# A two-layer sequence model: SiLU of B and C on ScalarE, store waits moved into the mixer's queue, row buffers set up earlier by GpSimd

## The reference

```
x = x + _L0_attn_ref(_layernorm(x), ...)      # decayed linear attention, gate, output product
x = x + _L0_ffn_ref(_layernorm(x), ...)       # router with top 8 of 64
x = x + _L1_attn_ref(_layernorm(x), ...)      # the mixer:
    proj = x @ in_proj_w.T                    # gate (8192), x (8192), B (1024), C (1024), dt (128)
    x, B, C = silu(causal depthwise conv of 4 taps + bias)
    L = exp(segsum(dt * A));  Y = (C B^T * L) @ (x * dt) + part of the earlier chunk + x * D
    out = (groupwise rms norm of Y * silu(gate)) @ out_proj_w.T
x = x + _L1_ffn_ref(_layernorm(x), ...)       # low-rank experts, top 16 of 64
```

## Time and profile before

| what | value |
|---|---|
| median of 3 runs | 2722.26 us (2721.75 to 2727.92) |
| the profiled execution, its time | 2725.14 us |
| the profiled execution, its span in the trace | 2723.4 us |
| TensorE matmul busy | 2566.6 us, 94% |
| VectorE, GpSimd, ScalarE busy | 69%, 54%, 50% |
| chain that ended last | TensorE 47%, VectorE 4%, "issue" 4%, GpSimd 2%, ScalarE 2% |

### The profile page before, as it was taken

How to read it: one execution, slowest core, us unless ns; L and a number is a source line. 1 busy time by engine, 2 the same in 40 slices (tenths; PEclk the granted TensorE clock), 3 DMA queues, 4 the chain that set the end, 5 groups by cost and what they waited for, 6 DMA issues and landing times.

```text
span 2723.4 us, 59094 instructions
## 1 busy us (share of the span) xinstructions
PE 2566.6 (94%) x19678; PEld 2041.8 (75%) x19678; DVE 1877.7 (69%) x2744; ACT 1349.5 (50%) x2481; POOL 1460.6 (54%) x1428
## 2 busy tenths in 40 slices
PE   4999999999999679799999999999999999999989
PEld 3778787787787456677777777777777777777777
DVE  5675666766757679757667777587576677775874
ACT  3434434434334255456564664665565646656621
POOL 1654655556546113457556656576575566575720
PEclk8999999999999879899999999999999999999999
DMA  2010010110110023211111111101111111111011
GB/s 89 24 50 29 32 46 24 40 40 23 47 36 12 15 93 112 72 45 38 50 33 58 34 42 50 36 31 50 45 37 51 33 54 34 45 49 38 18 47 47
DMA packets 72663, 119.04 MB, mean 44 GB/s; under 512 B 10310, under 2 KB 22214, under 8 KB 72373
## 3 DMA queue, kind: packets, MB, share of 16 engines
q1 hardware_dynamic: 72388, 115.61, 12.9%
HBM read 102.92 MB, written 12.65 MB: 42 GB/s over the span
## 4 chain that ended last, share of the span: by engine, by line
PE 47%; DVE 4%; issue 4%; POOL 2%; ACT 2%; DVEq 0%; ACTq 0%; POOLq 0%; DMA 0%; SPq 0%
PE proj L216 10%; PE proj L218 10%; PE proj L217 10%; PE core_y L1406 5%; PE core_o L1412 2%; PE turned L250 2%; DVE mx_acc L1192 2%; PE turned L1433 2%; PE decay L1465 1%; PE mx_decay L1465 1%; POOL mx_acc L1674 1%; PE mx_decay L216 1%; PE mx_decay L217 1%; PE mx_decay L218 1%; POOL mx_th L1671 1%
## 5 line engine op out<-in xcount | busy, mean ns | idle before, releaser
L216 PE MATMUL proj<-slab_hi,XTL 128*128 128x512 f32 x816 | 354.6, 435 | 0.0
L199 DVE TENSOR_TENSOR slab_lo<-slab_raw,slab_hi 128x512 fp32r<-128x512 f32 (+2 forms) x272 | 256.8, 956 | 133.5 <-ACT slab_hi L190 108.1
L216 PE MATMUL proj<-XTH,slab_lo 128*128 128x512 f32 x736 | 299.6, 407 | 44.8 <-PEq L81 18.5
L218 PE MATMUL proj<-slab_hi,XTH 128*128 128x512 f32 x816 | 320.2, 392 | 0.0
L217 PE MATMUL proj<-slab_lo,XTH 128*128 128x512 f32 x816 | 318.4, 390 | 0.0
L218 PE MATMUL proj<-XTH,slab_hi 128*128 128x512 f32 x736 | 291.9, 397 | 0.0
L217 PE MATMUL proj<-XTL,slab_hi 128*128 128x512 f32 x736 | 291.4, 396 | 0.0
L1688 POOL TENSOR_TENSOR mx_gate<-mx_gate,mx_hd 128x512 f32<-128x512 f32 x128 | 171.2, 1337 | 156.0 <-DVE mx_hd L1602 145.0
L216 PE MATMUL proj<-slab_hi,mx_otl 128*128 128x512 f32 x576 | 242.0, 420 | 0.0
L218 PE MATMUL proj<-slab_hi,mx_oth 128*128 128x512 f32 x576 | 227.7, 395 | 0.0
L217 PE MATMUL proj<-slab_lo,mx_oth 128*128 128x512 f32 x576 | 227.2, 394 | 0.0
(11 more groups left out here) (353 smaller groups left out, 6750.3 us busy)
## 6 DMA issues: line engine op xcount, KB each, us to landing
slab_raw<-in_w_gate SPq DMA_DIRECT2D x64, 256.0 KB, 3.0
slab_raw<-in_w_out SPq DMA_DIRECT2D x64, 256.0 KB, 3.0
slab_raw<-in_w_x SPq DMA_DIRECT2D x60, 256.0 KB, 3.6
slab_raw<-in_w_q SPq DMA_DIRECT2D x32, 256.0 KB, 3.0
slab_raw<-in_w_g SPq DMA_DIRECT2D x32, 256.0 KB, 3.0
slab_raw<-in_w_o SPq DMA_DIRECT2D x32, 256.0 KB, 2.9
bc_scratch<-bc_acc SPq DMA_DIRECT2D x32, 256.0 KB, 2.0
slab_raw<-in_w_bc SPq DMA_DIRECT2D x20, 256.0 KB, 4.3
```

Source lines behind the costliest of these rows:

```text
L199: op = nc.vector.tensor_tensor(K.SL[par][:, c, 0:width], K.RAW[c][:, 0:width], hi, ALU.subtract)
L216: nc.tensor.matmul(to[:, 0:bh.shape[-1]], al, bh, start=(c == 0), stop=False)
L218: mm = nc.tensor.matmul(to[:, 0:bh.shape[-1]], ah, bh, start=False, stop=(c == KC - 1))
```

## The change

B and C: ScalarE applies its own `Silu` to the tile in place, with a scale of 2. The tanh buffers, VectorE's and GpSimd's instructions for it and one wait of ScalarE go. The waits for the stores move from the end of the block to the mixer's list of SyncE, behind three loads. The row buffers `K.RHS` and `K.LHS` and the staging tile for `head_rows` are allocated with the layer, and GpSimd sets them up in the decay stage. ScalarE, VectorE and GpSimd then wait for three loads (`mx_ld`, 48) at the mixer's start.

```
 decay_phase:
+    if layer:
+        stage = sb("row_stage", [15, HH1 * SEQ])
...
             sp.dma_start(K.CB[:, :], d["conv_b"]).then_inc(S["bc_ld"], 16)
+            sp.dma_start(stage[:, :], d["head_rows"].rearrange("p h n -> p (h n)")).then_inc(S["mx_rows"], 16)
...
+    if layer:
+        @block.gpsimd
+        def _(pool):
+            for i in range(2):
+                alone(pool)
+                nc.gpsimd.memset(K.LHS[i][:, :, :], 0.0)
+                alone(pool)
+                nc.gpsimd.memset(K.RHS[i][:, :, :], 0.0).then_inc(S["mx_zero"], 1)
+            pool.wait_ge(S["mx_zero"], HEAD + 2)
+            pool.wait_ge(S["mx_rows"], HEAD + 16)
+            for i in range(2):
+                alone(pool)
+                nc.gpsimd.memset(K.LHS[i][0:15, :, :], 1.0)
+                alone(pool)
+                rows_set = nc.gpsimd.tensor_copy(K.RHS[i][0:15, :, :].rearrange("p h n -> p (h n)"), stage[:, :])
+            rows_set.then_inc(S["mx_set"], 1)
 bc_phase:
-        for k in range(4):
-            sp.wait_ge(S[f"bc_st{k}"], HEAD + 16 * 8)
-        sp.wait_ge(S["dt_st_1"], HEAD + 16 * 6)
...
                         act.wait_ge(S["bc_tap"], HEAD + 3 * n)
-                        act.wait_ge(S["bc_cm"], HEAD + n - 2)
-                        nc.scalar.activation(th[(u - 1) % 2][:, :], acc[(u - 1) % 4][:, :], ACT.Tanh).then_inc(S["bc_th"], 1)
+                        nc.scalar.activation(acc[(u - 1) % 4][:, :], acc[(u - 1) % 4][:, :], ACT.Silu, scale=2.0).then_inc(S["bc_cm"], 1)
...
-                    if u > 0 and u % 2 == 0:
-                        dve.wait_ge(S["bc_th"], HEAD + n)
-                        dve.wait_ge(S["bc_cm"], HEAD + n - 1)
-                        nc.vector.scalar_tensor_tensor(a, th[(u - 1) % 2][:, :], 1.0, a, ALU.add, ALU.mult).then_inc(S["bc_cm"], 1)
...
-    @block.gpsimd
-                nc.gpsimd.tensor_tensor(w, w, a, ALU.mult).then_inc(S["bc_p"], 1)
-                nc.gpsimd.tensor_tensor(a, w, a, ALU.add).then_inc(S["bc_cm"], 1)
 mixer_phase, SyncE:
-            sp.dma_start(HS[0:15, 0:4, :].rearrange("p t n -> p (t n)"), d["head_rows"].rearrange("p h n -> p (h n)")).then_inc(S["mx_ld"], 16)
+            for k in range(4):
+                sp.wait_ge(S[f"bc_st{k}"], HEAD + 16 * 8)
+            sp.wait_ge(S["dt_st_1"], HEAD + 16 * 6)
 mixer_phase, ScalarE:
-            act.wait_ge(S["mx_set"], HEAD + 1)
+            act.wait_ge(S["mx_ld"], HEAD + 48)
 mixer_phase, VectorE:
-            dve.wait_ge(S["mx_ld"], HEAD + 64)
-            for i in range(2):
-                nc.vector.memset(LHS[i][:, :, :], 0.0)
-                nc.vector.memset(RHS[i][:, :, :], 0.0).then_inc(S["mx_zero"], 1)
...
-            rows_set.then_inc(S["mx_set"], 1)
+            dve.wait_ge(S["mx_ld"], HEAD + 48)
```

More of the change, by code:

```diff
@@ L149, in build @@
             K.CW = mem.enter_context(nc.sbuf_tensor("conv_w", [P, (INTER + 2 * G1 * N1) // P, 4], F32))
+            K.RHS = [mem.enter_context(nc.sbuf_tensor(f"mx_g_rows{i}", [P, HH1, SEQ], BF16)) for i in range(2)]
+            K.LHS = [mem.enter_context(nc.sbuf_tensor(f"mx_j_rows{i}", [P, 2, SEQ], BF16)) for i in range(2)]
             K.CB = mem.enter_context(nc.sbuf_tensor("conv_b", [P, (INTER + 2 * G1 * N1) // P], F32))
@@ L166 @@
        "at_mask", "at_y", "at_th", "at_gate", "at_yg", "at_sq", "at_ss", "at_p", "at_x", "at_rl"]
-    + ["bc_ld", "bc_a", "bc_tap", "bc_th", "bc_p", "bc_cm", "bc_st0", "bc_st1", "bc_st2", "bc_st3"]
-    + ["mx_ld", "mx_zero", "mx_set", "mx_bc", "mx_row0", "mx_row1", "mx_a", "mx_tap", "mx_th", "mx_cm", "mx_hsT", "mx_pt", "mx_hs",
+    + ["bc_ld", "bc_a", "bc_tap", "bc_cm", "bc_st0", "bc_st1", "bc_st2", "bc_st3"]
+    + ["mx_ld", "mx_rows", "mx_zero", "mx_set", "mx_bc", "mx_row0", "mx_row1", "mx_a", "mx_tap", "mx_th", "mx_cm", "mx_hsT", "mx_pt", "mx_hs",
        "mx_pof", "mx_cb", "mx_bt", "mx_d", "mx_e", "mx_m", "mx_xc", "mx_hd", "mx_xd", "mx_y", "mx_yb",
@@ L1202, in bc_phase @@
     acc = [mem.enter_context(nc.sbuf_tensor(f"bc_acc{i}", [P, HALF], F32)) for i in range(4)]
-    th = [mem.enter_context(nc.sbuf_tensor(f"bc_th{i}", [P, HALF], F32)) for i in range(2)]
     block = K.block
@@ L1263, in _ @@
                         conv_taps(nc, dve, acc[u % 4], banks[u % 4], [K.CW[:, ds(blk + u % 4, 1), k] for k in range(3)], S["bc_tap"], 3 * n)
-                    if u > 0 and u % 2 == 0:
-                        dve.wait_ge(S["bc_th"], HEAD + n)
-                        dve.wait_ge(S["bc_cm"], HEAD + n - 1)
-                        a = acc[(u - 1) % 4][:, :]
-                        nc.vector.scalar_tensor_tensor(a, th[(u - 1) % 2][:, :], 1.0, a, ALU.add, ALU.mult).then_inc(S["bc_cm"], 1)
-    @block.gpsimd
-    def _(pool):
-        with pool.Fori(0, 2) as i:
-            for u in range(0, 16, 2):
-                n = 16 * i + u
-                pool.wait_ge(S["bc_th"], HEAD + n + 1)
-                pool.wait_ge(S["bc_cm"], HEAD + n)
-                alone(pool)
-                a, w = acc[u % 4][:, :], th[u % 2][:, :]
-                nc.gpsimd.tensor_tensor(w, w, a, ALU.mult).then_inc(S["bc_p"], 1)
-                pool.wait_ge(S["bc_p"], HEAD + 8 * i + u // 2 + 1)
-                alone(pool)
-                nc.gpsimd.tensor_tensor(a, w, a, ALU.add).then_inc(S["bc_cm"], 1)
     K.slab += 4
@@ L1336, in mixer_phase @@
         K.OTL = [sb(f"otl{i}", [P, KC, P], F32R) for i in range(2)]
-        RHS = [sb(f"g_rows{i}", [P, HH1, SEQ], BF16) for i in range(2)]
-        LHS = [sb(f"j_rows{i}", [P, 2, SEQ], BF16) for i in range(2)]
+        RHS, LHS = K.RHS, K.LHS
         tri = sb("tri", [P, P])
@@ L1571, in _ @@
         def _(dve):
-            dve.wait_ge(S["mx_ld"], HEAD + 64)
-            for i in range(2):
-                nc.vector.memset(LHS[i][:, :, :], 0.0)
-                nc.vector.memset(RHS[i][:, :, :], 0.0).then_inc(S["mx_zero"], 1)
-            dve.wait_ge(S["mx_zero"], HEAD + 2)
-            for i in range(2):
-                nc.vector.memset(LHS[i][0:15, :, :], 1.0)
-                rows_set = nc.vector.tensor_copy(RHS[i][0:15, :, :].rearrange("p h n -> p (h n)"), HS[0:15, 0:4, :].rearrange("p t n -> p (t n)"))
-            rows_set.then_inc(S["mx_set"], 1)
+            dve.wait_ge(S["mx_ld"], HEAD + 48)
             def half(g, s, last):
@@ L1657, in _ @@
         def _(pool):
-            pool.wait_ge(S["mx_ld"], HEAD + 64)
+            pool.wait_ge(S["mx_ld"], HEAD + 48)
             def half(g, s, last):
```

## The result

The change makes the kernel some 0.2% faster: 2718.43 us (median of 11 runs, 2709.66 to 2722.7) against 2723.64 us (11 runs). The ratio that is estimated from all of these runs is 0.9975 with a 95% interval of 0.9966 to 0.9984. The medians differ by 5.2 us, the ratio stands for a gain of 6.8 us (4.4 to 9.3), and 13.2 were forecast. The time lies above the range on record. The profiled execution took 2718.86 us.

A forecast was written before the change was run, and what follows sets the result against it. TensorE bounds the kernel, losing time in VectorE-paced B and C, at that stage's end and at the mixer's start. Gains 8.0 + 2.6 + 6.6 = 17.2, less 4.0, give 13.2: 2722.26 - 13.2 = 2709 us, range 2703 to 2717.

The forecast's parts named there:

- Term 1: B and C stage: Silu on ScalarE cuts the slab period from 25.1 to 22.7, a gain of 8.0 us.
- Term 2: End of B and C: last taps to TensorE's restart goes from 4.65 to 2.06, a gain of 2.6 us.
- Term 3: Mixer's start: TensorE's restart to slot 5 goes from 24.76 to 18.16, a gain of 6.6 us.
- Term 4: Behind rstd: GpSimd's setup takes turns with VectorE and delays the last xn_c, 4.0 us lost (0 to 11.7).
- The layout: Norm's xn_c: instruction-by-instruction order of GpSimd's fills and copies against VectorE's, last xn_c moved from 957.54 to 961.6.
- setup dear: Rival, GpSimd's setup behind rstd: near the two-input price, gain only 5.5 to 8, 2714 to 2717 us; chance 0.10.
- The drain: Rival, ScalarE's table loads: each switch costs its drain too, 2.8 us more, 2712 us; chance 0.04.

The follow-up runs named there:

- e3: Kernel before with only Silu on ScalarE in B and C; 2717.4 us against 2723.61, ratio 0.9978.
- e5: Kernel before with only the row setup moved to GpSimd behind rstd; 2726.95 us against 2723.61, ratio 1.0013.
- e8: Kernel before with store waits on the mixer's queue and GpSimd's row setup behind the norm, without Silu; 2717.22 us against 2725.3, ratio 0.9969.
- e6: Changed kernel with only four fills behind rstd, 15-row fills and copies moved to B and C; 2713.49 us, ratio 0.9959 to before.
- e7: Changed kernel with xn_c of norm "c" made by scalar_tensor_tensor, the slow form; 2714.82 us, ratio 0.9960 to before.
- e1: Changed kernel with GpSimd's row setup waiting for the B and C stage; 2710.8 us, again 2712.28 us, ratios 0.9950 and 0.9958 to before.
- e2: Changed kernel with GpSimd's row setup behind the norm's last XTL, at the decay stage's start; 2710.88 us, ratio 0.9951 to before.
- e9: e1 with ScalarE's two passes over B and C written out instead of looped; 2713.24 us, ratio 0.9949 to before.

## Why the prediction was wrong

Counted as it was, to the start of slot 5: 949.43 to 1125.33 is 175.9 before, 949.34 to 1116.95 is 167.6 after, a gain of 8.3.

- **Term 1, the pace of B and C: right.** 8.0 forecast, 8.0 measured (104.2 to 96.2; 104.7 and 95.6 in the other profiles), with the 24.0 period where it was put and 22.5 against 22.7 for the next one. SiLU costs tanh's 0.63, and a load 1.28 with nothing behind it. e3 shows it without the other parts. (As printed, the four parts of this term add up to 7.9, and its 0.22 is a step that the rows give as 0.25. Neither matters to the result.)
- **Term 2, the end of the stage: right.** 2.6 forecast, 2.8 measured.
- **Term 3, the mixer's start: the right number, in part by luck.** Restart to slot 5 is 18.28 against 18.16 forecast, the gain 6.5 against 6.6. ScalarE's table load starts 4.55 after the restart and its first split 5.85, where 5.6 was forecast and 5.8 allowed. But the load is not free here, as e5 and e8 show (17.25 and 17.42 without it). The sum hid its cost of about 1, because it took 14.06 for TensorE's way to slot 4 from the first profile. The other two profiles of before have 12.75: their matmuls are at half rate until 3.7 behind the restart, those of the first until 6.3.
- **Term 4, GpSimd's setup: the step that failed.** 4.0 forecast for the last `xn_c`, 7.5 measured there (8.1 to 15.6), and 9.0 from `rstd` to `dtd` (18.9 to 27.9). The other profiles have 8.0 and 8.1 for the two. The mechanism was the right one, the engines taking turns for whole instructions: e6 and e7 show it, and that of the two forms of `xn_c` only the faster is held by a fill. Its size was wrong in three places. The fills are 1.80 to 2.08 and 0.53 to 0.79, where 1.2 and 0.3 were taken from a one-input row of another kind; the copies were cheaper than their 2.3, at 1.94 and 2.06. The layout had the copies fall partly beside low parts that read PSUM, where a longer set of fills pushed all four of the first `xn_c` back so far that both copies met an `xn_c` or a low part with two SBUF inputs; that makes 7.5 of the 9.0. And 1.5 more came from a neighbour not priced at all, TensorE's clock. Its matmuls of the decay stage are 0.63 long, at half rate, from 968.05 to 973.34 in the changed kernel, and from 960.52 to 962.82 before. e5, e6 and e7 have it as long as that too. The second profile of the changed kernel has not, and there only some 0.2 come on top of the `xn_c`, so this part is not there in every run.
- **Outside the terms.** 13.2 less 5.0 for term 4, and 0.1 more from the other terms, is the 8.3 of the trace, where the medians differ by 5.2. The interval of the ratio, 4.4 to 9.3 us, holds both. The forecast of 2709 also stood on the first median of before, 2722.26 from 3 runs, where 11 runs have 2723.64. So with term 4 put right the forecast would have been 2714 to 2715, inside the range, and the 3.1 us that are left are not outside that interval. e1 leaves 3.6 and 5.9 of its 16.4 unseen in the same way (172.5, the mean of the three sums of before, less 156.0), e2 3.0, e9 5.4, e3 2.5, e7 0.8, e8 0.1, and e6 none. The profiled executions of before (2725.14, 2730.72, 2726.57) all lie above the medians, and the runs differ in how long the clock is at half around TensorE's stops. The rests of the table have a mean of 1603.8 in the three profiles of before and of 1602.6 in the two of the changed kernel, so for the changed kernel no lasting loss behind slot 4 is seen. In e1, e2 and e9, which come to slot 4 earliest, the mean of the four is 1606.0 (e9 has its own 2.2 in it). Whether these 2 us are chance, or the mixer is lastingly longer behind an early start, stays open.

The rival "setup dear" named what happened, with its gain of 5.5 to 8, at the two-input price. That price is not what the runs show: a fill has its own, 0.88 ns an element (1.80 for 2048), and what was dear was the order in which the instructions met. Its layout had the last `xn_c` 11.7 late, where 7.5 and 8.0 were measured. The rule from the Trainium skill, "SBUF — State Buffer", Who interferes with whom, that the prediction cited, a two-port mode and any GpSimd instruction exclude each other while two SBUF inputs are held by a read only, agrees with e1, e2, e6 and e7 in both halves: `xn_c` in the 0.48 form 6.03 instead of 1.92 beside fills, a low part 0.68 beside a fill and 1.94 beside a copy (e1). The drain that the Trainium skill, "ScalarE: Activation LUTs", What ACT_TABLE_LOAD costs, has behind a load is again not there: after 1051.01 and 1.28 the next instruction starts at 1052.30.

The best of these kernels is the change with GpSimd's setup at another place: e1, 2711.5 us over ten runs and 12.8 and 10.5 us faster than before, or e2, 2710.88 us over five, with the same work in all. Runs can't tell the two apart, and neither has the setup for nothing: a copy costs e1 1.3 in the first slab of B and C, and e2 1.3 at `dtd`.

## What to carry to other kernels

Work that is "hidden" on an idle engine still has to be placed: look which VectorE instructions run in that window, and in which mode. Beside a chain of fast tensor_scalar on the critical path even fills cost nearly what they last (4.1 in e6), while beside taps that read PSUM or subtractions of two tensors fills cost nothing here, and two copies cost 1.3 in e1 and e2 instead of 3.4 with the 15-row fills. And lay a contended stretch out with the longest price for each neighbour too, since a longer one doesn't only add its own length but changes what the next ones meet. A table load is to be priced again at every place where an engine waits for what stands behind it: of the two that mattered here the forecast's sum counted one.

## What the runs showed of the hardware

- GpSimd's fill of 128x2048 bf16 takes 1.80, of 128x512 0.52 (e1); a copy of 15x2048 from f32 to bf16 takes 1.88, as dear on 15 partitions as a fill on 128. Where they met `xn_c` in the changed kernel they took up to 2.08, 0.79 and 2.06.
- Four tensor_scalar of 0.48 each went from 1.92 to 6.03 beside fills (e6) and to 7.71 and 8.17 beside fills and a copy (the changed kernel's two profiles); four scalar_tensor_tensor with two SBUF inputs took 2.74 beside fills, and one of them 2.12 beside a copy (e7).
- In the same program TensorE's clock is at half for different lengths of time at the same place: 0.91 against 0.74 over the same 20 us of the router stage, and half rate until 6.3, 3.7 and 3.7 behind the mixer's restart in the three profiles of before.
- With a loop of ScalarE's in the B and C stage written out (e9, one profile), every second half group of the mixer was 0.3 us longer, without a change to the mixer.
- e9 has three of the four table loads of B and C less than e1 and gains 1.7 to 1.9, of which 1.4 at the gap between slabs 2 and 3. The same load of 1.28 costs about 1 at the mixer's start (18.2 to 18.3 with it, 17.25 and 17.42 without).
